# The first group of an attention block made on chip, and the modulations moved into that block's drain

## The chip, the cores and the metric

The kernel runs on one core of a Trainium2 chip. The metric is device microseconds (us) of one execution; three executions are summed up by their median. The profile is one further execution, recorded by the hardware profiler.

## The reference

The input is `x` of 16 x 128 x 256 (batch, channels D, positions T) and a mask `cond_2048` of 16 x 256. Two layers are added to `x` in turn; all arithmetic is float32.

```python
def _L0_cond_ref(x, mask, Wq, Wo):          # first layer
    xt = jnp.transpose(x, (0, 2, 1))
    q = xt @ Wq.T
    qh = q.reshape(B, T, NH, dk).transpose(0, 2, 1, 3)      # 8 heads of 16
    scores = scale * jnp.einsum('bhqd,bhkd->bhqk', qh, qh)
    logits = (scores * cmask + (1.0 - cmask) * NEG) * rmask
    attn = jax.nn.softmax(logits, axis=-1)
    ctx = jnp.einsum('bhqk,bhkd->bhqd', attn, qh)
    out = ctx.transpose(0, 2, 1, 3).reshape(B, T, D) @ Wo.T
    return jnp.transpose(out, (0, 2, 1))

def _L1_cond_ref(x, timestep_embed, ada_w, ada_b, ...):     # second layer
    ada = (timestep_embed @ ada_w + ada_b)[:, None, :]      # timestep_embed is the mask array
    shift1, scale1, gate1, shift2, scale2, gate2 = jnp.split(ada, 6, axis=-1)
    x1 = _ln(x) * (1.0 + scale1) + shift1
    ...                                     # 16 heads of attention, gate1, _ln, scale2, shift2, a gelu layer, gate2

x = x + _L0_cond_ref(x, cond_2048, L0_cond_Wq, L0_cond_Wo)
x = x + _L1_cond_ref(x, cond_2048, ...)
```

## The kernel before

The program has two blocks with a barrier between them. The first, `first_block`, is the first layer; the second, `layers`, is the second layer, in float32 products that are split into a high and a low part. The change touches only the first.

The first block works on 8 groups of two batch entries each. A group has 4 units; a unit is two heads (s = 0, 1) of both entries (b = 0, 1), so there are 32 units (`UNITS`). For a unit n the engines do:

- PE: `scores(n, b)` (L401) from the stacked rows `KS` and `QS` into the PSUM tensor `ring`; later `shift(n, b)` (L413), which adds the negative maxima through an identity; later `pv(n, kt)` (L425), the product of the exponentials with the values `V`, into `pair`.
- DVE: `maxima(n, b)` (L602), two reductions.
- ACT: `exponentials(n, b)` (L539), two activations into `pt`.

The stacked rows hold, for each head, three parts of 16 rows and a row (two in the layout) for the mask, so that one product over 49 rows gives queries times keys to float32 accuracy and the masking. They are made by a round trip: POOL multiplies x with the mask and splits the product in a high part `xh` and a low part `xl` (`masked(g)`, L333 to L340); PE projects them with Wq (`project(g)`, three products in L672); ACT copies the high part of the result (`queries(g)`, L522), DVE the low part (`low(g)`, L597); SP writes both to HBM (`gather(g)`, L262 and L264) and reads them back into the rows of `KS` and `QS` (`spread(g)`, six transfers in L280 for the queries, four in L273 for the mask rows). `values(g)` (L378, ACT L529) makes V.

A group's end is a tail that is spread over the following units: `sums` (ACT L549), transposes (PE L471), division by the sums (DVE L640, L647), transposes (L478), a copy (ACT L568), the product with Wo (L483) and the addition to `X` (DVE L656). For the last group there are no more units, so the tail stands alone; that end, with the first row norms of the second layer (`deviations`, `normal_rows`, L149 to L168, turned by PE in L116), is called the drain here.

Beside that the first block prepares the second one. SP loads the 12 chunks of the second layer's weights into `stage` (L288); ACT and POOL split each half chunk into `w_hi` (L573) and `w_lo` (L355), one half chunk in each of units 0 to 23. The modulations (`ada`, six vectors for every entry) are 24 products of 16 columns on PE (L387), in four parts: two ahead of the first scores and two in unit 0. `modulated` (L607 to L617) finishes them on DVE in unit 1. The weights of the modulations lie in `late` and in half of `pt`; therefore `exponentials` of units 0 and 1 and the first `sums` wait for all four parts (`pe_ada`).

Each engine runs its own instructions in program order; SP's are the loads and stores, all on one queue. The order is written out by hand: every engine has a loop over n in which the calls above stand. An instruction that waits holds back all that is behind it on its engine. The head of SP's list before the change is x[0:2], mask(0), Wq, the constants, cond, Wo, mask(1), x[2:4], the modulations' weights (1.5 MB), the mask rows, gather(0), the biases, spread(0), x[4:16] (1.5 MB), mask(2), gather(1), two weight chunks, and then per group `spread(g + 1)`, `mask(g + 3)`, `gather(g + 2)` and two weight chunks.

Of the kernel before, what the change touches and what calls it, by code (L numbers as in the profile page):

```python
# [12 lines left out]
P = 128  # L13
# [159 lines left out]
def first_block(nc, sem, sb, x, cond, Wq, Wo, ada_w, ada_b, qkv_w, qkv_b, out_b, ffn_b1, ffn_b2,  # L173
# [5 lines left out]
    LAST = 4 * (NGR - 1) + 8  # L179
    LQ, LG = 10 * 16, 3 * 16  # L180
    vbank, tbank = psum[0], psum[1]
    O = psum[2]
    with ExitStack() as ctx:
# [25 lines left out]
        first = pt[:, 0, :, :, :].rearrange("p a s n -> p (a s n)")  # L209
        wqo = first[:, 0:2 * P].rearrange("p (i n) -> p i n", i=2)  # L210
        cnd = first[0:B, 512:512 + DIM]
        bias_rows = first[0:BIASES, 1024:1024 + P]
        aw = [late[:, 0:6 * DIM], pt[:, 1, :, :, :].rearrange("p a s n -> p (a s n)")[:, 0:6 * DIM]]

        l_cst, l_small, l_w, l_x0, l_x1, l_x, l_ada = (sem(n) for n in (
            "l_cst", "l_small", "l_w", "l_x0", "l_x1", "l_x", "l_ada"))
# [22 lines left out]

        def tail_of(n, lag):  # L240

            g, r = divmod(n - lag, 4)
            return g if r == 0 and 0 <= g < NGR else None

        with nc.Block() as block:

            @block.sync
            def _(sp):
                def mask(g):

                    wait(sp, pool_x, g - 1)
# [3 lines left out]
                def gather(g):  # L255

                    q = qd[g % 2]
                    if g >= 2:
                        sp.wait_ge(l_q[g % 2], LQ * (g // 2))
                    sp.wait_ge(act_q1, g + 1)  # L260
                    for c in (0, 2):
                        sp.dma_start(q[:, c], qh[:, :].bitcast(F32)).then_inc(l_qd[g % 2], 16)  # L262
                    sp.wait_ge(dve_ql, g + 1)
                    sp.dma_start(q[:, 1], ql[:, :].bitcast(F32)).then_inc(l_qd[g % 2], 16)  # L264

                def spread(g):
# [9 lines left out]
                    sp.wait_ge(l_qd[g % 2], LG * (g // 2 + 1))  # L276
# [15 lines left out]
                sp.dma_start(wqo[:, 0, :], Wq).then_inc(l_w, 16)  # L292
                sp.dma_start(cst[:, :], consts).then_inc(l_cst, 16)
                sp.dma_start(cnd, cond).then_inc(l_w, 16)
                sp.dma_start(wqo[:, 1, :], Wo).then_inc(l_w, 16)
                mask(1)
                sp.dma_start(X[:, 2:4, :], x[2:4].rearrange("b p d -> p b d")).then_inc(l_x1, 16)
# [10 lines left out]
                sp.wait_ge(l_nb, 16)  # L308
                spread(0)
                sp.dma_start(X[:, 4:B, :], x[4:B].rearrange("b p d -> p b d")).then_inc(l_x, 16)  # L310
                mask(2)
                gather(1)
                weights(0)
                weights(1)
                for g in range(NGR):
                    if g + 1 < NGR:
                        spread(g + 1)
# [1064 lines left out]
```

## Time and profile before

| | us |
|---|---|
| median of 3 executions | 802.7 (802.21 to 804.07) |
| the profiled execution, its own time | 802.39 |
| its span, first to last instruction | 800.6 |
| first block, start to the barrier | 0 to 205.6 |
| first scores (unit 0) | 30.33 |
| first scores of unit 4 (group 1) | 58.24 |

PE is busy for 747.2 us of the span (93%), ACT for 436.6, DVE for 385.5 and POOL for 144.8. In a row of the time line the first number is the start, the second the time from there to the end of the last of the instructions that are merged in the row, then come engine, line, operation, the tile written and what it was made from, and the count. Brackets hold how long the engine was idle before it and what ended that.

### The profile page before, as it was taken

Reading aid. Unit: us, or ns where it says so; the run is one execution under the profiler, and the core shown is the slowest. Engines: PE = TensorE matmul, PEld = TensorE weight load, DVE = VectorE, ACT = ScalarE, POOL = GpSimd, SP = SyncE. Lnnn points to the kernel's source line nnn. Section 1 sums busy time; section 2 is a strip of 40 time slices with the busy share of each in tenths; the row PEclk is TensorE's granted clock in tenths of the full one; section 3 lists DMA queues with packets and bytes.
Section 4 is the critical chain, followed back from the end, with each engine's and each line's share of the span. In section 5 each row is a group of like instructions: output and inputs, shape, how many; then the busy total and the mean of one; then the engine's idle time right before and its main releaser. Section 6 shows DMA issues by size and latency. Waiting matters only on the chain.

```text
span 800.6 us, 12914 instructions
## 1 busy us (share of the span) xinstructions
PE 747.2 (93%) x4737; PEld 615.9 (77%) x4737; DVE 385.5 (48%) x782; ACT 436.6 (55%) x1189; POOL 144.8 (18%) x136
## 2 busy tenths in 40 slices
PE   3689999997699999999999999999999999899997
PEld 2555555554598888888888888888888888778886
DVE  1155666666234543444545444545444345545444
ACT  1056776765357454555564555565544566647553
POOL 4133444200033111111111111111111122200000
PEclk9999999999899999999999999999999999999999
DMA  6999988740433221221221221212222223220001
GB/s 196 244 155 188 200 206 192 138 64 1 131 119 103 69 80 68 66 79 67 67 80 66 66 75 59 76 66 65 79 80 66 80 93 105 80 79 31 29 21 53
DMA packets 68851, 75.69 MB, mean 95 GB/s; under 512 B 4040, under 2 KB 48064, under 8 KB 68800
## 3 DMA queue, kind: packets, MB, share of 16 engines
q1 hardware_dynamic: 68800, 75.01, 35.1%
q8 instruction: 32, 0.52, 0.3%
q14 instruction: 19, 0.16, 0.1%
HBM read 47.96 MB, written 27.03 MB: 94 GB/s over the span
## 4 chain that ended last, share of the span: by engine, by line
PE 69%; DVE 3%; ACT 2%; DMA 1%; issue 0%; DVEq 0%; SPq 0%; ACTq 0%
PE bank L672 27%; PE pair L672 14%; PE ring L672 13%; PE ring L958 7%; PE pair L944 6%; PE ring L116 1%; DVE x1l L1186 1%; ACT x1h L1046 1%; PE ring L977 0%; ACT probs L1065 0%; DMA x1f<-in_L_cond_ffn_w_dram 0%; PE ring L913 0%; DVE ol L1219 0%; DVE pB L1197 0%; DMA turned<-pB 0%
## 5 line engine op out<-in xcount | busy, mean ns | idle before, releaser
L1065 ACT ACTIVATE probs<-pair,nm 128x128 f32<-128x128 f32 x256 | 98.5, 486 | 183.1 <-DVE nm L1208 183.1
L1321 POOL TENSOR_TENSOR probs<-probs,rinv 128x512 f32<-128x512 f32 x64 | 66.7, 1042 | 356.6 <-DVE rinv L1216 356.6
L672 PE MATMUL bank<-x1h,w_hi 128*128 128x512 f32 x256 | 112.1, 438 | 5.6 <-DVE x1l L1186 5.5
L602 DVE TENSOR_REDUCE mx<-ring 128x2 fp32r<-128x512 f32 x128 | 80.1, 683 | 64.2 <-PE ring L401 64.2
L672 PE MATMUL bank<-x1l,w_hi 128*128 128x512 f32 x256 | 101.5, 396 | 0.0
L672 PE MATMUL bank<-x1h,w_lo 128*128 128x512 f32 x256 | 101.2, 395 | 0.0
L539 ACT ACTIVATE pt<-ring 128x512 f32<-128x512 f32 x128 | 70.1, 594 | 44.2 <-PE ring L413 44.0
L1239 DVE COPY Vv<-pair 128x512 f32<-128x512 f32 x64 | 44.2, 691 | 80.4 <-PE pair L672 80.4
L672 PE MATMUL pair<-w_hi,x1l 128*128 128x256 f32 x256 | 72.7, 284 | 0.0
L672 PE MATMUL pair<-w_lo,x1h 128*128 128x256 f32 x256 | 72.4, 283 | 0.0
L672 PE MATMUL pair<-w_hi,x1h 128*128 128x256 f32 x256 | 72.2, 282 | 0.0
L944 PEld LDWEIGHTS pair<-K,Q 128*128 128x128 f32 x512 | 67.0, 191 | 5.3
L958 PEld LDWEIGHTS ring<-pT,Vv 128*128 128x128 f32 x512 | 66.8, 191 | 5.1
L944 PE MATMUL pair<-K,Q 128*128 128x128 f32 x512 | 67.6, 275 | 0.0
L958 PE MATMUL ring<-pT,Vv 128*128 128x128 f32 x512 | 67.3, 274 | 0.0
L1219 DVE SCALAR_TENSOR_TENSOR ol<-ring,bias,oh 128x512 fp32r<-128x512 f32 x64 | 48.0, 750 | 32.2 <-ACT oh L1074 32.2
L1208 DVE TENSOR_REDUCE nm<-pair 128x4 f32<-128x512 f32 x64 | 43.7, 682 | 40.2 <-PE pair L944 40.0
L1216 DVE RECIPROCAL rinv<-sums 128x4 f32<-128x4 f32 x64 | 11.4, 178 | 102.4 <-ACT probs L1065 102.4
L672 PEld LDWEIGHTS bank<-x1h,w_hi 128*128 128x128 f32 x256 | 49.1, 192 | 12.8 <-issue 5.8
L672 PEld LDWEIGHTS bank<-x1h,w_lo 128*128 128x128 f32 x256 | 48.7, 190 | 11.0
L1065 ACT ACTIVATION_READ_ACCUMULATOR probs<-pair,nm 128x1 f32 x256 | 56.1, 219 | 0.0
L672 PE MATMUL ring<-oh,wo_hi 128*128 128x512 f32 x128 | 51.0, 399 | 3.5 <-DVE ol L1219 3.4
(175 smaller groups left out, 1476.0 us busy)
## 6 DMA issues: line engine op xcount, KB each, us to landing
turned<-pB SPq DMA_DIRECT2D x63, 256.0 KB, 2.0
pT<-turned SPq DMA_DIRECT2D x63, 256.0 KB, 2.8
QS<-qd SPq DMA_DIRECT2D x16, 384.0 KB
stage<-in_L_cond_qkv_w_dram SPq DMA_DIRECT2D x12, 512.0 KB, 7.6
qd<-qh SPq DMA_DIRECT2D x16, 256.0 KB
KS<-qd SPq DMA_DIRECT2D x16, 256.0 KB
mb<-in_cond_dram SPq DMA_DIRECT2D x8, 256.0 KB, 10.4
qd<-ql SPq DMA_DIRECT2D x8, 256.0 KB
```

The lines of the kernel that those rows point to most:

```text
L116: last = nc.tensor.transpose(bank[:, (2 * k + b) * P:(2 * k + b + 1) * P], xn(2 * half + b)[:, k * P:(k + 1) * P], ident)
L539: nc.scalar.activation(pt[:, n % 2, b, s, :], ring[:, 2 * b + s, :], ACT.Exp, scale=DK ** -0.5).then_inc(act_exp, 1)
L602: dve.tensor_reduce(mx[:, 2 * b + s, :], ring[:, 2 * b + s, :].rearrange("p (k q) -> p k q", k=2), AX_X, ALU.max, negate=True).then_inc(dv ...
L672: last = nc.tensor.matmul(bank, w(k), x(k), start=(start and i == 0), stop=(stop and i == len(terms) - 1))
L944: last = nc.tensor.matmul(Sb[:, t], Q[:, h % 2, t], K[:, h % 2, t], start=True, stop=True)
L958: last = nc.tensor.matmul(Ob[:, b * T:(b + 1) * T], V[:, ho // 2 % 2, b, h % 2 * DH:(h % 2 + 1) * DH], pT[:, h % 2, :, b, :], start=True, ...
L1065: last = nc.scalar.activation(plain(probs)[:, t] if direct else probs[:, :, b, :].rearrange("p c a -> p a c"), Sb[:, t] if direct else Sb[ ...
L1208: dve.tensor_reduce(nm[:, h % 2, :], Sb[:, :].rearrange("p (b k) -> p b k", b=GB), AX_X, ALU.max, negate=True).then_inc(dve_mx, 1)
L1216: dve.reciprocal(rinv[:, h % 2, :], sums[:, h % 2, :]).then_inc(dve_ri, 1)
L1219: dve.scalar_tensor_tensor(ol[:, :], Ob[:, :], qkvb[:, 2, ho:ho + 1], oh[:, :].bitcast(F32), ALU.add, ALU.subtract).then_inc(dve_ol, 1)
L1239: dve.tensor_copy(V[:, hn // 2 % 2, 2 * (hn % 2):2 * (hn % 2) + 2, :], Vb[:, :].rearrange("p (b d) -> p b d", b=2)).then_inc(dve_v, 1)
L1321: pool.tensor_tensor(w, w, r, ALU.mult).then_inc(pool_p, 1)
```

## The change

- Group 0 takes no round trip. DVE multiplies x[0:2] with the mask and splits it (`x0m`, `x0h`, `x0l`). ACT and DVE copy each head's 16 columns of Wq three times into a stack `ws_h`, `ws_l` of 8 x 64 columns. PE's new `stack(j)` gives the stacked rows of unit j directly: four products of 512 columns into `pair`, the first of which puts the mask row in; ACT makes `h0` from it, and two operations of DVE write `QS` and `KS`. `stack(0)` stands ahead of the first scores, `stack(n + 1)` in units 0 to 2. Ahead of them PE runs 6, 4 and 3 products with zeros.
- `gather(0)`, `spread(0)` and `masked(0)` are gone. `project(1)` and `values(0)` stand in unit 0, with their parts on ACT and DVE.
- Wq, the constants, cond and Wo are loaded from ACT's queue. x comes in four loads, [0:2], [2:4], [4:8] and [8:16], of which the last stands behind `spread(1)`.
- The weight splits are done in units 2 to 25 (`SPLIT0 = 2`); one weight chunk is loaded between `mask(g + 3)` and `gather(g + 2)`, the other one behind it.
- All four parts of the modulations and the turn of the biases stand behind the last product with V (n == UNITS), `modulated` one step later on DVE. Their weights and the biases are loaded at the end of SP's list, into `stage`, `xm` and half of `V`, when those are free.

```diff
+        x0h, x0l, ws_h, ws_l, one_h, zero, h0, mbr = (
+            w_hi[:, 6144 + 512 * i:6144 + 512 * (i + 1)] for i in range(8))
...
                 def mask(g):
 
-                    wait(sp, pool_x, g - 1)
+                    wait(sp, pool_x, g - 2)
+                    if g == 2:
+                        sp.wait_ge(dve_x0, 1)
+                        sp.wait_ge(act_mbr, 1)
...
-                for k in range(KT):
-                    sp.dma_start(aw[k], ada_w[k * P:(k + 1) * P, :]).then_inc(l_ada, 16)
                 sp.wait_ge(pool_nb, 1)
                 sp.dma_start(rowd.rearrange("t b d -> b t d"), rows[:, :, :]).then_inc(l_nb, 16)
-                gather(0)
+                sp.dma_start(X[:, 4:8, :], x[4:8].rearrange("b p d -> p b d")).then_inc(l_x2, 16)
+                mask(2)
+                gather(1)
+                weights(0)
+                sp.wait_ge(l_nb, 16)
+                spread(1)
+                sp.dma_start(X[:, 8:B, :], x[8:B].rearrange("b p d -> p b d")).then_inc(l_x, 16)
+                weights(1)
+                for g in range(NGR):
+                    if g and g + 1 < NGR:
+                        spread(g + 1)
+                    if g + 3 < NGR:
+                        mask(g + 3)
+                    if g and 2 * g + 1 < CHUNKS:
+                        weights(2 * g + 1)
+                    if g + 2 < NGR:
+                        gather(g + 2)
+                    if 2 * g + 2 < CHUNKS:
+                        weights(2 * g + 2)
+                sp.wait_ge(pool_lo, 2 * CHUNKS)
+                sp.dma_start(aw[0][0], ada_w[0:P, :]).then_inc(l_ada, 16)
...
+                sp.wait_ge(pool_x, NGR - 1)
+                sp.dma_start(aw[1][1], ada_w[P:2 * P, 8 * P:12 * P]).then_inc(l_ada, 16)
+                sp.wait_ge(pe_pv, 4 * (NGR - 1))
+                sp.dma_start(aw[1][0], ada_w[P:2 * P, 0:8 * P]).then_inc(l_ada, 16)
...
+                def zeros(count):
+
+                    for i in range(count):
+                        nc.tensor.matmul(ring[:, 0, :], zero[:, 0:P], zero, start=True, stop=True)
+
+                def stack(j):
+
+                    bank = O[:, min(j, 1), :]
+                    w = slice(j * P, (j + 1) * P)
...
+                    nc.tensor.matmul(bank, one_h[:, 0:P], mbr, start=True, stop=False)
...
+                    nc.tensor.matmul(bank, ws_h[:, w], x0h, start=False, stop=False)
...
+                    nc.tensor.matmul(bank, ws_l[:, w], x0h, start=False, stop=False)
...
+                    nc.tensor.matmul(bank, ws_h[:, w], x0l, start=False, stop=True).then_inc(pe_st, 1)
...
                 for n in range(LAST + 1):
                     if n < UNITS:
                         scores(n, 0)
-                    if n == 0:
-                        modulations(2)
                     if 0 <= n - 1 < UNITS:
                         shift(n - 1, 1)
+                    if n == 0:
+                        pe.wait_ge(act_set, 1)
+                        pe.wait_ge(dve_set, 1)
+                        project(1)
+                    if n < 3:
+                        stack(n + 1)
...
+                    if n == UNITS:
+                        pe.wait_ge(act_exp, 4 * UNITS)
+                        pe.wait_ge(l_small, 80)
+                        nc.tensor.transpose(ring[:, 1, 12 * B:12 * B + BIASES], bias_rows, ident[0:BIASES, 0:BIASES])
+                        pe.wait_ge(l_ada, 48)
+                        for part in range(4):
+                            modulations(part)
...
+                def stack(j):
+
+                    act.wait_ge(pe_st, j + 1)
+                    wait(act, dve_st, j)
+                    nc.scalar.activation(h0, O[:, min(j, 1), :], ACT.Identity, bias=cols[:, 1:2],
+                                         scale=cols[:, 0:1]).then_inc(act_h, 1)
...
+                def stack(j):
+
+                    dve.wait_ge(act_h, j + 1)
+                    h, bank = h0.bitcast(F32), O[:, min(j, 1), :]
+                    dve.scalar_tensor_tensor(QS[:, 0, j, :], h, cols[:, 2:3], bank, ALU.mult, ALU.add)
+                    dve.scalar_tensor_tensor(KS[:, 0, j, :], h, cst[:, C_AK:C_AK + 1], bank, ALU.mult,
+                                             ALU.add).then_inc(dve_st, 1)
```

PE's order up to the second half of unit 0's scores, before. `bank` is the PSUM bank of projections and modulations, L401 the scores:

```order
L435 MATMUL bank<-cst,pt 128x128 x2
L437 MATMUL bank<-cst,pt 128x16 x2
L672 MATMUL bank<-xh,wq_h 128x512
L672 MATMUL bank<-xl,wq_h 128x512
L672 MATMUL bank<-xh,wq_l 128x512
L378 MATMUL bank<-wT,X 128x128 x4
...
L446 MATMUL bank<-cst,pt 128x72
L387 MATMUL bank<-cndT,late 128x16
...
L401 MATMUL ring<-QS,KS 128x256 x4
```

And in the changed kernel (L411 are the products with zeros, L420 to L430 a stack, L446 the scores, L790 project(1)):

```order
L411 MATMUL ring<-w_hi 128x512 x6
L481 MATMUL bank<-cst,pt 128x128
L411 MATMUL ring<-w_hi 128x512 x4
L484 MATMUL ring<-cst,pt 128x128
L486 MATMUL ring<-cst,pt 128x16 x2
L411 MATMUL ring<-w_hi 128x512 x3
L420 MATMUL pair<-w_hi 128x512
L424 MATMUL pair<-w_hi 128x512
L427 MATMUL pair<-w_hi 128x512
L430 MATMUL pair<-w_hi 128x512
L446 MATMUL ring<-QS,KS 128x256 x4
L790 MATMUL bank<-xh,wq_h 128x512
```

The projection, the values and twelve of the modulation products have left the place ahead of the first scores; zeros and one stack stand there.

SP's list from the mask rows on, in the changed kernel:

```order
L314 DMA rowd<-rows 16x2x256
L315 DMA X<-in_x_dram 128x4x256
L272 DMA mb<-in_cond_dram 128x512
L281 DMA qd<-qh 8x16x512 x2
L283 DMA qd<-ql 8x16x512
L307 DMA stage<-in_L_cond_qkv_w_dram 128x1024
L292 DMA QS<-rowd 1x4x512 x2
...
L299 DMA QS<-qd 48x4x512
L321 DMA X<-in_x_dram 128x8x256
L307 DMA stage<-in_L_cond_qkv_w_dram 128x1024
L272 DMA mb<-in_cond_dram 128x512
L281 DMA qd<-qh 8x16x512 x2
```

The first pair of gather and spread in it belongs to group 1; no 1.5 MB load stands ahead of it any more, and 1 MB of x and a weight chunk stand behind it, ahead of gather(2).

PE's order in the drain, in the changed kernel (L470 the products with V, L514 and L521 the tail's transposes, L116 the turn of the normalized rows, L526 the product with Wo):

```order
L470 MATMUL pair<-pt,V 32x256 x8
L549 MATMUL ring<-cst,stage 128x72
L404 MATMUL ring<-cndT,stage 128x16
L404 MATMUL ring<-cndT,V 128x16
...
L404 MATMUL ring<-cndT,xm 128x16
L514 MATMUL bank<-cst,late 128x128 x4
L116 MATMUL bank<-cst,mb 128x128 x4
L116 MATMUL ring<-cst,mb 128x128 x4
L514 MATMUL bank<-cst,late 128x128 x4
L521 MATMUL bank<-cst,late 128x128 x4
L526 MATMUL bank<-late,wT 128x512
```

Before, the first L514 (then L471) followed the products with V directly; the 25 rows between are new there.

## Rows read from the trace of the kernel before

**Rows 1.** The page: TensorE's busy tenths in 40 slices of the span.
```profile
PE   3689999997699999999999999999999999899997
```

**Rows 2.** Time line of the start: spread(0), first scores, first weight split.
```profile
18.13 0.92 SPq L280 DMA_DIRECT2D KS<-qd  x2
...
30.33 0.79 PE L401 MATMUL ring<-QS,KS 49*128 49x256 f32 x4 [5.94 <-DMA QS<-qd]
...
40.22 0.62 ACT L573 CAST w_hi<-stage 128x512 fp32r<-128x512 f32 x1 [21.54 <-DMA stage<-in_L_cond_qkv_w_dram]
```

**Rows 3.** Time line, PE: the first scores of units 4, 8 and 12.
```profile
58.24 0.50 PE L401 MATMUL ring<-QS,KS 49*128 49x256 f32 x4
...
79.13 0.50 PE L401 MATMUL ring<-QS,KS 49*128 49x256 f32 x4
...
98.45 0.50 PE L401 MATMUL ring<-QS,KS 49*128 49x256 f32 x4
```

**Rows 4.** Time line of the drain, PE, DVE and ACT.
```profile
195.35 1.07 PE L425 MATMUL pair<-pt,V 128*32 128x256 f32 x16
...
199.74 0.66 PE L116 MATMUL bank<-cst,mb 128*128 128x128 f32 x4 [2.73 <-DVE mb L168]
...
204.63 0.69 DVE L656 TENSOR_TENSOR X<-bank,X 128x512 f32<-128x512 f32 x1 [2.55 <-PE bank L483]
...
205.63 1.51 ACT L1031 ACTIVATE x1f<-bank,ada 128x128 f32<-128x128 f32 x4 [2.21 <-PEq L245]
```

**Rows 5.** Time line of the start: durations on POOL, ACT and DVE.
```profile
4.52 1.26 POOL L333 TENSOR_TENSOR xm<-X,mb 128x512 f32<-128x512 f32 x1 [4.08 <-DMA mb<-in_cond_dram]
...
9.73 0.59 ACT L522 CAST qh<-bank 128x512 fp32r<-128x512 f32 x1 [2.58 <-PE bank L672]
...
18.71 0.69 DVE L597 TENSOR_TENSOR ql<-bank,qh 128x512 fp32r<-128x512 f32 x1 [7.67 <-ACT qh L522]
```

**Rows 6.** Time line, PE: products at the slow level, and the first fast one.
```profile
11.19 2.05 PE L378 MATMUL bank<-wT,X 128*128 128x128 f32 x8 [1.49 <-DVE ql L597]
...
14.57 0.63 PE L672 MATMUL bank<-xl,wq_h 128*128 128x512 f32 x1
...
14.99 0.63 PE L672 MATMUL bank<-xh,wq_l 128*128 128x512 f32 x1
...
42.60 1.22 PE L413 MATMUL ring<-identr,mx 128*128 128x256 f32 x4
...
44.66 1.08 PE L425 MATMUL pair<-pt,V 128*32 128x256 f32 x8 [0.84 <-ACT pt L539]
...
51.09 0.39 PE L672 MATMUL bank<-xh,wq_l 128*128 128x512 f32 x1
```

**Rows 7.** Stretches: busy us by engine (count), granted clock, DMA share, GB/s.
```profile
80.00:90.00 10.00, 8.84 (x76) 5.14 (x76) 6.86 (x14) 6.79 (x13) 4.98 (x5) 1.00 0.91 197
...
210.00:212.00 2.00, 2.00 (x6) 1.54 (x6) 0.00 (x0) 0.00 (x0) 0.00 (x0) 0.50 1.03 326
```

**Rows 8.** The page's groups: busy, mean ns of one, idle before.
```profile
L1219 DVE SCALAR_TENSOR_TENSOR ol<-ring,bias,oh 128x512 fp32r<-128x512 f32 x64 | 48.0, 750 | 32.2 <-ACT oh L1074 32.2
```

**Rows 9.** Time line: two like operations of DVE, and POOL's beside them.
```profile
44.99 0.19 DVE L613 TENSOR_TENSOR gb<-ada,bias 128x32 f32<-128x32 f32 x1
45.10 1.27 POOL L355 TENSOR_TENSOR w_lo<-stage,w_hi 128x512 fp32r<-128x512 f32 x1 [2.92 <-ACT w_hi L573]
45.22 1.20 DVE L615 TENSOR_TENSOR gb<-ada,bias 128x32 f32<-128x32 f32 x1
```

**Rows 10.** Time line, SP's queue: the first of spread(7)'s transfers.
```profile
157.68 0.91 SPq L280 DMA_DIRECT2D KS<-qd  x2
```

**Rows 11.** Stretches, as in rows 7: where that spread ends.
```profile
168.00:169.00 1.00, 1.00 (x13) 0.46 (x12) 0.44 (x1) 1.00 (x2) 0.00 (x0) 1.00 0.68 102
169.00:170.00 1.00, 1.00 (x11) 0.69 (x7) 1.00 (x3) 0.05 (x1) 0.00 (x0) 1.00 0.11 18
```

**Rows 12.** Time line, PE: the first and last products of modulation parts 0, 1.
```profile
19.15 0.54 PE L387 MATMUL bank<-cndT,late 128*128 128x16 f32 x2
...
23.80 0.59 PE L387 MATMUL bank<-cndT,pt 128*128 128x16 f32 x2
```

More of the change, by code:

```diff
@@ L179, in first_block @@
     LAST = 4 * (NGR - 1) + 8
+    SPLIT0 = 2
     LQ, LG = 10 * 16, 3 * 16
@@ L307, in _ @@
                     row += n
[L308 to L317, printed above, removed]
-                    if g + 3 < NGR:
-                        mask(g + 3)
-                    if g + 2 < NGR:
-                        gather(g + 2)
-                    for c in (2 * g + 2, 2 * g + 3):
-                        if c < CHUNKS:
-                            weights(c)
+                sp.wait_ge(pool_x, NGR - 1)
+                sp.dma_start(aw[1][1], ada_w[P:2 * P, 8 * P:12 * P]).then_inc(l_ada, 16)
+                sp.wait_ge(pe_pv, 4 * (NGR - 1))
+                sp.dma_start(aw[1][0], ada_w[P:2 * P, 0:8 * P]).then_inc(l_ada, 16)
             @block.gpsimd
@@ L372, in values @@
                 def values(g):
-                    taken = min(g + 2, NGR) if g else 1
+                    taken = min(g + 1, NGR - 1)
                     wait(pe, act_q1, taken)
@@ L544, in sums @@
                     wait(act, pe_pv, 4 * g + 2 * half + 2)
-                    if g == 0:
-                        act.wait_ge(pe_ada, 4)
-                    else:
+                    if g:
                         wait(act, pe_oT, 2 * g + half - 1)
                     nc.scalar.copy(oT[:, half, :], O[:, half, :]).then_inc(act_o, 1)
-                queries(0)
-                values(0)
-                queries(1)
+                act.wait_ge(dve_zero, 5)
+                stack(0)
                 for n in range(LAST + 1):
@@ L556, in _ @@
                         exponentials(n - 1, 1)
+                    if n == 0:
+                        queries(1)
+                    if n < 3:
+                        stack(n + 1)
                     if n % 4 == 2 and n // 4 + 2 < NGR:
@@ new lines, in _ @@
+                TINY = 2.0 ** -12
+                dve.memset(zero.bitcast(F32), 0.0).then_inc(dve_zero, 1)
+                dve.memset(w_hi[:, 7168:8192].bitcast(F32), 0.0).then_inc(dve_zero, 1)
+                dve.memset(one_h[:, 0:P].bitcast(F32), 0.0).then_inc(dve_zero, 1)
+                dve.wait_ge(dve_zero, 3)
+                ones = one_h[:, 0:P].bitcast(F32).rearrange("p (s r) -> p s r", s=2)[:, :, ROWS_ONE:ROWS_ONE + 1]
+                dve.memset(ones, TINY / P).then_inc(dve_zero, 1)
@@ L629, in _ @@
                         maxima(n, 0)
-                    if n == 1:
-                        modulated()
+                    if n == 0:
+                        low(1)
+                    if n < 3:
+                        stack(n + 1)
                     if n % 4 == 2 and n // 4 + 2 < NGR:
```

203 lines of the change are left out of this document (125 added, 78 removed).

## Prediction

> **What bounds the kernel now.** I first read the page's busy line by tenths of the span: TensorE works nearly throughout, and only the first block (the first ten of 40 slices) has holes, at its start and its end [rows 1]. Then I read the time line of that block, from its start, for what ended each wait. The first scores start at 30.33 us and wait there for DMA: spread(0), issued from 18.13 on, took until then [rows 2]. What stands before 30 us is one round trip of the first queries through HBM. A second wait follows: ScalarE stands in front of its first weight split until 40.22 us, because the load of the weights is queued behind everything else, and the exponentials of unit 0 are behind that split in program order [rows 2]. So unit 4, the first of group 1, starts only at 58.24 us. From there a group takes 20.9 us (58.24 to 79.13) and then 19.3 (79.13 to 98.45) [rows 3]; nothing in this steady part waits for a spread. The block ends in a drain: the last products with V from 195.35 on, the normalized rows turned at 199.74, the last addition to X at 204.63; at 205.63 all engines pass to the second block [rows 4], which the change leaves alone. What group 0 saves is therefore worth its full size at the end, if the later groups keep their pace, less what is added to the drain.
>
> **Group 0 up to its first scores.** Removed: gather(0), spread(0), the POOL part masked(0). Added: a chain PE, ACT, DVE. The four loads that now go through ACT's queue start at once; the row nearest to them is POOL's first product, which had its two inputs at 4.52 with the same kind of loads in flight [rows 5]. I take Wq and the constants at about 4 us, x and its mask at 4.8. Then: transpose of Wq and its end, 4.6; ScalarE's ws_h, at most the 0.59 of a 512-column copy, 5.2; VectorE's ws_l, at most the 0.69 of a 512-column operation [rows 5], 5.8; x0m, x0h and x0l, 0.69 each at most, 7.8. Beside this TensorE runs 13 zero products of 512 columns, which start 0.42 us apart at the slow level, 1.2 GHz [rows 6], 5.5 us in all, and the transposes of Wo and the conditions; started at 1.4 (after one memset of 512 columns, which has no row on VectorE and is taken as no more than 0.69), it is through them at 8.4. (The level is told by durations, 0.63 against 0.39; the granted clock shows it as 0.50 where it has fallen before [rows 7].) So the zeros hide VectorE's chain, and not the other way round. stack(0) is four such products: 10.1, its result seen at 10.3. ScalarE's h0 0.59 [rows 5]: 11.0. Two scalar_tensor_tensor of 0.75 [rows 8]: 12.6. First scores at **12.7** instead of 30.33.
>
> One thing lies in the way: VectorE's x0m and x0l run while POOL makes masked(1). In the trace, two like operations of VectorE differ: 0.19 us alone, and 1.20 when started 0.12 after a POOL product of 1.27, ending with it [rows 9]. By this row one VectorE step can be held 1.3 us; the zeros cover that much (9.7 is when TensorE wants x0l, 7.8 when it is ready). If two steps are held, scores start at 13.4. The Trainium skill, SBUF — State Buffer, "Who interferes with whom", says that a VectorE operation with two SBUF inputs and a GpSimd one that reads SBUF exclude each other for the whole operation, whichever starts first; by that rule the total would be up to 0.7 us above mine. The trace agrees in the one place where it shows it.
>
> **Units 0 to 3.** At the fast level a normal unit takes 4.8 (19.3 / 4) [rows 3]. Units 0 to 2 now also hold stack(n+1): four products on TensorE, one h0 on ScalarE (0.59; the weight split of the same size leaves units 0 and 1) and 1.5 on VectorE, which has to be done before the next scores and stands between the two pairs of maxima. I add 0.6 for each, since VectorE, with four maxima of 0.65 and these 1.5, is then the tightest engine: 5.4. Unit 0 also has project(1), queries(1), low(1) and values(0), mostly at the slow level: 6.6. Unit 2 has project(2), queries(2) and low(2): 5.9; unit 3 values(1): 5.5. Sum 23.4, so unit 4 could start at 36.1.
>
> Its rows must be there. gather(1) is issued when queries(1) is done, 15.4, and low(1), 16.1; nothing is in flight then but x[4:8] and a mask, so its 768 KB are written by 20.5. spread(1) takes 11.5 us, as the last spread does when it is alone: issued 157.68, the transfer gone in the slice 169 to 170 [rows 10, 11]. It lands at 32, four before it is wanted. Unit 4 starts at **36.1** instead of 58.24: **22.1 us gained**. Its weights are in front too: weights(0) goes out before spread(1), so ScalarE's wait of 21.54 [rows 2] is gone; what is late next is weights(1) with 1 MB of x ahead of it, wanted only in unit 4.
>
> **Group 1 and after.** spread(2) follows 1.75 MB of x, weights and mask and the 768 KB of gather(2), behind spread(1); at the 326 GB/s of a plain load [rows 7] these take 5 and 3 us: 32 + 5 + 3 = 40, landing at 53 with weights(2) ahead. Unit 8 asks at 36.1 + 19.3 = 55.4. So it just fits; the margin is 2.4. Later spreads are issued at the same place of a group as now (the split that the second load waits for has moved by two units, and the order of the loads with it). The 20.9 of group 1 hold 1.6 over the steady 19.3; I count half of that as gone, **0.8**. Units 24 and 25 now hold a weight split each (0.59 to 0.62 on ScalarE), of which I count **0.5** on the path.
>
> **The drain.** Added on TensorE behind the last product: the transpose of the biases (0.3) and 24 products of 16 columns. At the slow level such a product starts every 0.43 (19.15 to 23.80: the first and the last of twelve rows of two records each, a product a row) [rows 12], 10.3 us in all; at the fast level half, 5.2. They are hidden only by the hole before 199.74, where TensorE waits 2.73 for the normalized rows [rows 4], and then in part, since the turn of group 7's first half, which now comes after them, has its partner on VectorE: 195.35 + 1.0 + 0.3 + 5.2 = 201.8 for the end of the products, 202.3 for that turn, 203.0 for its VectorE part. Then VectorE makes the modulations, seven small steps of 0.19 or somewhat more [rows 9] with a wait between them, 1.7 us without POOL beside it, up to 204.7; the second half's VectorE part ends at 205.4. From that end to the last addition VectorE idles 2.55 now [rows 4] (transpose, ScalarE's copy, product) and the addition takes 0.69: 208.6 for 205.3, **3.3 us lost**. At the slow level 8.5 would be lost. The last product leaves TensorE at the fast level, and the small ones came in the trace only at the slow one, so I take **4.5**. Their loads (ada in three pieces, five of biases) wait for the last split, for masked(7) and for unit 27, all over 15 us before: nothing.
>
> Sum, on the profiled execution of 802.39 (0.3 below the median of 802.7): 802.39 - 22.1 - 0.8 + 0.5 + 4.5 = **784.5**. To put both ends: without any gain in group 1, with the drain at 8.5, 789.3; with units 0 to 3 at 4.8 each, so that unit 4 starts as its rows land, at 32, and with the drain at 3.3, 779.2.
>
> **Rivals.**
> *A, TensorE stays at the slow level through group 0.* For: after the zeros it has nothing to do for 2.4 us while ScalarE and VectorE finish stack(0); and in the trace the first 512-column product of 0.39 comes at 51.09 [rows 6]. Against: it came there after six us without a hole, 44.66 on, and from 12.7 on the new order has no hole either. Price: scores 0.79 [rows 2], shift 1.22, products with V 1.08 [rows 6], twice each, is 6.2, and a stack 1.7; with two projections of 1.3 and two value products of 2.05 [rows 6], without unit 0's products with V, 34.6 for four units by durations, some 31 by starts (a row's end lies some 0.1 behind the next one's start): unit 4 at 43.7, **792**.
> *B, the wait moves from group 0 to group 1.* spread(1) or spread(2) lands later than asked. For: DMA is busy 0.91 in the steady part [rows 7], and the margin at unit 8 is small. Past the margin each us late is one us of time; with spread(2) 8 to 10 late, **790 to 792**. This is also the case on the other side: if spread(1) lands no sooner than spread(1) of before, just ahead of 58.24, then group 0's gain is all waited away and the drain's 4.5 and the 0.5 remain, **807**. It decides from a landing at 53 on, 21 later than I work out. Against: 3 MB (x and ada) that stood before it in the queue are behind it now.
> *C, the modulations in the drain run at the slow level.* In the trace products of 16 columns came at the slow level alone [rows 12]. Price 8.5 for 4.5: **788.5**.
> *D, the first scores come as late as before*, the change not doing what it says: nothing in the order makes them wait for HBM any more; not given a chance of its own.
>
> **How the numbers follow.** Forecast (779 to 788) 0.60; A 0.13; B up to 795 0.09, B past the point 0.03; C 0.13; better than 779, 0.02. Predicted 784.5. The range, 779 to 793, takes in the forecast with its ends, C, A at its price and most of B. A measurement of this kernel can tell about 0.2% (1.6 us) from no change: faster by more 0.96, within 0.01, slower 0.03.
>
> **What would show it.** Right: first scores at 12 to 14 us; unit 4 at 34 to 39 with its idle time ended by ScalarE or VectorE, not by DMA; a start of unit 8 some 19 to 20 later; the 16-column products right behind the last product with V, 5 to 7 us long; the second block some 17 to 19 earlier than 205.63. Wrong: scores of unit 4 or 8 released by DMA (B); 512-column products still 0.42 apart after 20 us (A); 16-column products 0.43 apart in the drain (C); anything else in the second block than a shift.

## The result and the profile after

The changed kernel takes 791.39 us (median of 4 runs, 789.09 to 792.2) beside 802.46 for the kernel before on the same chip: ratio 0.9839, interval 0.9806 to 0.9872. The profiled execution took 792.2 us, span 790.0. Forecast were 784.5 and 779 to 793: right in sign, inside the range, 6.9 us too low, and outside the 779 to 788 of the forecast without its rivals. Lines of after: scores L446, stack L420 to L430, modulations L404.

The page's busy tenths, against [rows 1]:
```profile
PE   7799999986999999999999999999999999899997
```
Of the hole at the start a shallow one is left; the one at the end of the first block is still there.

The start, time line, against [rows 2, 5, 8]:
```profile
5.98 0.47 PE L481 MATMUL bank<-cst,pt 128*128 128x128 f32 x1 [1.59 <-DMA cst<-stack_constants]
...
8.19 2.20 DVE L730 CAST w_hi<-pt 128x512 fp32r<-128x512 f32 x1
...
8.84 1.26 POOL L353 TENSOR_TENSOR xm<-X,mb 128x512 f32<-128x512 f32 x1
...
10.07 0.63 PE L420 MATMUL pair<-w_hi 128*128 128x512 f32 x1
...
10.43 0.98 DVE L732 TENSOR_TENSOR w_hi<-pt,w_hi 128x512 fp32r<-128x512 f32 x1
...
12.35 0.78 ACT L575 ACTIVATE w_hi<-pair,cols 128x512 fp32r<-128x512 f32 x1 [4.33 <-PE pair L430]
...
14.62 0.50 PE L446 MATMUL ring<-QS,KS 49*128 49x256 f32 x4 [2.37 <-DVE KS L700]
```
The constants come at 5.98, VectorE's cast of x0h takes 2.20 while POOL works beside it, and the first scores start at 14.62 instead of 30.33.

Group 1's rows, SP's queue and PE, and the starts of units 8 and 12 [rows 3]:
```profile
18.07 0.62 SPq L283 DMA_DIRECT2D qd<-ql  x1
...
24.94 0.81 SPq L299 DMA_DIRECT2D KS<-qd  x2
...
38.95 0.50 PE L446 MATMUL ring<-QS,KS 49*128 49x256 f32 x4 [3.70 <-DMA QS<-qd]
...
60.96 0.51 PE L446 MATMUL ring<-QS,KS 49*128 49x256 f32 x4
...
79.78 0.50 PE L446 MATMUL ring<-QS,KS 49*128 49x256 f32 x4
```
TensorE was ready for unit 4 at 35.25 and waited 3.70 for its rows. Group 1 then takes 22.0 (38.95 to 60.96), longer than the 20.9 before; the stretches (columns as in [rows 7]) show the clock there:
```profile
35.00:40.00 5.00, 1.30 (x16) 0.83 (x8) 1.51 (x3) 0.28 (x2) 0.50 (x1) 0.99 1.10 228
40.00:45.00 5.00, 4.17 (x28) 1.88 (x26) 1.73 (x4) 3.08 (x6) 1.27 (x2) 0.50 0.91 346
45.00:50.00 5.00, 5.00 (x30) 3.38 (x26) 2.37 (x6) 2.43 (x5) 4.39 (x4) 0.50 0.57 174
50.00:55.00 5.00, 5.00 (x43) 3.18 (x43) 3.32 (x6) 3.27 (x7) 0.27 (x1) 0.99 1.04 157
```
After the idle stretch the granted clock is 0.50 for ten us. From unit 8 on a group takes 18.8 (60.96 to 79.78), the last 18.3; before it was 18.3 to 19.3.

The drain, against [rows 4]:
```profile
175.78 1.07 PE L470 MATMUL pair<-pt,V 128*32 128x256 f32 x16
...
179.54 0.37 PE L404 MATMUL ring<-cndT,stage 128*128 128x16 f32 x2
...
180.16 0.59 PE L404 MATMUL ring<-cndT,stage 128*128 128x16 f32 x2
...
184.43 1.09 PE L514 MATMUL bank<-cst,late 128*128 128x128 f32 x4
...
190.75 2.07 PE L526 MATMUL bank<-late,wT 128*128 128x512 f32 x2 [0.68 <-ACT late L641]
...
192.86 0.69 DVE L772 TENSOR_TENSOR X<-bank,X 128x512 f32<-128x512 f32 x1 [3.96 <-PE bank L526]
...
197.84 0.77 PE L790 MATMUL bank<-x1h,w_hi 128*128 128x512 f32 x1 [5.02 <-DVE x1l L1304]
```
The stretches:
```profile
175.00:180.00 5.00, 5.00 (x47) 3.66 (x46) 3.73 (x17) 1.68 (x4) 0.00 (x0) 0.98 0.00 0
180.00:190.00 10.00, 9.13 (x42) 8.39 (x41) 3.02 (x14) 0.00 (x0) 0.00 (x0) 0.50 0.00 0
```
The modulations start 0.22 apart and from 179.7 on 0.43 apart. The last addition to X stands 17.1 behind the last products with V; before it was 9.3, with the granted clock at 1.00 throughout. The second block's first product (209.61 before) starts 11.8 earlier, the span ends 10.6 earlier.

### The profile page after: what moved, and what is told of

The parts are those of the page before. It is cut to its first block, busy times and chain, and to the rows that moved or that the text cites. A ratio compares the mean times of both kernels' runs of the same rounds, so it can differ in the third digit from the quotient of the medians.

```text
span 790.0 us, 12978 instructions
## 1 busy us (share of the span) xinstructions
PE 756.6 (96%) x4763; PEld 621.5 (79%) x4763; DVE 394.5 (50%) x801; ACT 439.5 (56%) x1194; POOL 142.5 (18%) x133
## 4 chain that ended last, share of the span: by engine, by line
PE 70%; DVE 3%; ACT 2%; DMA 1%; issue 0%; DVEq 0%; SPq 0%; ACTq 0%
PE bank L790 27%; PE pair L790 14%; PE ring L790 13%; PE ring L1076 7%; PE pair L1062 7%; PE ring L116 1%; DVE x1l L1304 1%; ACT x1h L1164 1%; PE ring L1095 0%; ACT probs L1183 0%; DMA x1f<-in_L_cond_ffn_w_dram 0%; PE ring L1031 0%; DVE ol L1337 0%; DVE pB L1315 0%; DMA turned<-pB 0%
## 5 line engine op out<-in xcount | busy, mean ns | idle before, releaser
L790 PE MATMUL bank<-x1h,w_hi 128*128 128x512 f32 x256 | 112.1, 438 | 5.6 <-DVE x1l L1304 5.5
L790 PE MATMUL bank<-x1l,w_hi 128*128 128x512 f32 x256 | 101.5, 396 | 0.0
L790 PE MATMUL bank<-x1h,w_lo 128*128 128x512 f32 x256 | 101.3, 396 | 0.0
L790 PE MATMUL pair<-w_hi,x1l 128*128 128x256 f32 x256 | 72.8, 284 | 0.0
L790 PE MATMUL pair<-w_lo,x1h 128*128 128x256 f32 x256 | 72.6, 283 | 0.0
L790 PE MATMUL pair<-w_hi,x1h 128*128 128x256 f32 x256 | 72.3, 282 | 0.0
L790 PEld LDWEIGHTS bank<-x1h,w_hi 128*128 128x128 f32 x256 | 49.1, 192 | 13.6 <-issue 6.6
L790 PEld LDWEIGHTS bank<-x1h,w_lo 128*128 128x128 f32 x256 | 48.6, 190 | 11.0
L458 PEld LDWEIGHTS ring<-identr,mx 128*128 128x128 f32 x256 | 37.6, 196 | 22.7 <-issue 13.4
```

The lines of the kernel that those rows point to most:

```text
L458: last = nc.tensor.matmul(out, mx[:, 2 * b + s, qt:qt + 1].to_broadcast([P, P]), identr[:, None, :].to_broadcast([P, 2, P]), start=False, ...
L790: last = nc.tensor.matmul(bank, w(k), x(k), start=(start and i == 0), stop=(stop and i == len(terms) - 1))
```

## The experiments

Each kernel is the changed one with the edit shown. Times are given by the ratio to the kernel before on the same chip, to be held against 0.9839; most intervals overlap with its own, so what decides is the trace, and where two ratios don't overlap this is said. A spread's time is counted from its first issue (L299 in the changed kernel), which is when its gather has landed, to the end of TensorE's wait (in c2, where TensorE doesn't wait, to the end of SyncE's). The four kernels under "All together" are called c1 to c4, in their order.

**POOL held back.**
```
 def masked(g):
     wait(pool, pool_x, g - 1)
+    if g == 1:
+        pool.wait_ge(dve_x0, 3)
```


> GpSimd's mask product and splits of group 1 wait until VectorE has finished its own split of group 0's rows; nothing else is changed. Theory (the cast that took 2.20 us on VectorE was held up by GpSimd's work beside it): the cast falls to 0.3 to 0.9 us, the low part from 0.98 to 0.7 or less, and the first scores start at 13.2 to 13.9 instead of 14.62; group 1's projection may then wait for GpSimd, to 15.5. The time falls by 0 to 1 us only if the rows of group 1 are not what group 1 waits for; since they are, 791 to 791.5. Rival (the cast waits for something else, the page's duration is not a conflict): it stays above 1.8 us and the first scores at 14.6.

Ratio 0.9791 (0.9735 to 0.9848). The time line's cast, first scores:
```profile
7.91 0.50 DVE L732 CAST w_hi<-pt 128x512 fp32r<-128x512 f32 x1
...
13.37 0.50 PE L448 MATMUL ring<-QS,KS 49*128 49x256 f32 x4 [2.37 <-DVE KS L702]
```
The cast falls from 2.20 to 0.50, the first scores come 1.25 earlier, and POOL's part ends when it did (12.6). The expectation that nothing reaches the end was wrong: the gather starts 1.25 earlier too, the rows land at 35.90 after a wait of 2.05, and unit 8 starts at 56.83, 4.1 earlier. Of the 3.05 by which the rows land earlier the earlier gather explains 1.25; the spread took 12.2 instead of 14.0 with the same transfers in the same order, and no run shows why. First scores differ too among the seven kernels that have the changed kernel's start (14.00 to 14.62), so that the hold's price lies between 0.6 and 1.25.

**Order of SyncE's loads.**
```
+sp.dma_start(X[:, 8:B, :], ...)
+weights(0)
+weights(1)
 gather(1)
-weights(0)
 sp.wait_ge(l_nb, 16)
 spread(1)
-sp.dma_start(X[:, 8:B, :], ...)
-weights(1)
```


> SyncE's order alone: the load of X[8:16] and the first two weight chunks are issued ahead of the gather of group 1 instead of among and behind its transfers; they then fall into the stretch 10 to 17 in which the queues stand idle. Theory (the rows of group 1 land late because the transfers compete): they land by 34 to 36 instead of 38.9, the wait of TensorE ahead of group 1 shrinks from 3.7 to under 1 us, the clock doesn't fall at 40, group 1 takes 19 to 20 us instead of 22.0, and the time falls by 4 to 6 us, to 785.5 to 787.5. Rival (the spread of the stacked rows is slow by itself, 2 KB rows into few partitions): it lands at 37 or later, the gain is under 2 us, time 789.5 or more.

Ratio 0.9799 (0.9744 to 0.9855). Time line, PE:
```profile
38.24 0.50 PE L446 MATMUL ring<-QS,KS 49*128 49x256 f32 x4 [2.14 <-DMA QS<-qd]
```
Unit 4 still waits 2.14; the rival is right, the spread took 13.4 from its issue at 24.86 with the loads out of its way.

**Zero products in the wait.**
```
+if n == 4:
+    pe.wait_ge(act_exp, 4 * 3 + 2)
+    zeros(14)
 if n < UNITS:
     scores(n, 0)
```


> 14 products with the zero tile are added ahead of group 1's first scores, in the time in which TensorE waits there for the rows; nothing else is changed. Theory (the idle wait, not the wait's length, lets the clock fall at 39.9): the granted clock of 40 to 50 is near 1 instead of 0.50, group 1 takes 19 to 20 us instead of 22.0, and unit 8's first scores come 2 to 3 us earlier than 60.96, with the time at 788.5 to 789.5. Rival (group 1 is held by the transfers of group 2's rows, whatever the clock): unit 8's first scores stay at 60 to 61 and the time at 791 to 792.

Ratio 0.9815 (0.9767 to 0.9863). The clock is 1.00 from 40 to 45 but falls after it (0.78 and 0.53 in the next two stretches of 5 us), and group 1 takes 22.8: ScalarE stood 1.46 us in front of a weight split whose chunk was queued behind 1 MB of x (1.44 in the changed kernel, at 42.92). So I repeated it with the two loads swapped:
```
-sp.dma_start(X[:, 8:B, :], ...)
 weights(1)
+sp.dma_start(X[:, 8:B, :], ...)
```


> The changed kernel with the 14 products with the zero tile ahead of group 1, as in the run that added them alone, and SyncE's second weight chunk issued ahead of X[8:16] instead of behind it. Theory (that run gained little because ScalarE, in its in-order queue ahead of the exponentials, then waited 1.46 us for that chunk, and the clock fell in the idle time that followed): no wait of ScalarE for a weight chunk in group 1, the clock near 1 from 40 to 55, group 1 in 19 to 20.5 us instead of 22 to 22.8, and the time 788 to 789. Rival (group 1 is bound by something else, as group 2's rows): ScalarE's wait goes, and group 1 still takes 21.5 us or more, time 790 to 792.

Ratio 0.9846 (0.9793 to 0.9898). Stretches, and unit 8's first scores:
```profile
40.00:45.00 5.00, 4.06 (x37) 2.47 (x38) 2.93 (x5) 3.37 (x7) 1.18 (x1) 1.00 0.93 331
45.00:50.00 5.00, 4.55 (x43) 2.98 (x42) 3.64 (x9) 3.66 (x8) 4.45 (x5) 1.00 0.74 187
```
```profile
60.26 0.50 PE L446 MATMUL ring<-QS,KS 49*128 49x256 f32 x4 [2.12 <-DMA QS<-qd]
```
No wait of ScalarE, the upper clock throughout, and group 1 needs 18.7 of its own (39.41 to 58.14). Of the gain in group 1, 2.12 is waited away at unit 8: the theory was right for group 1, the rival for the time.

**No zeros at the start** (`zeros(6)`, `zeros(4)` and `zeros(3)` taken out).

> The 13 products with the zero tile at the start are left out. Theory (they raise the clock, and are otherwise hidden): the products of the first stack run at the lower level, about 0.43 each and more instead of 0.21 to 0.43, units 0 to 3 run slow at their start, unit 4's first scores come at the time of the rows anyway (38.5 to 39.5) since group 1 waits for them, and the time is the same within 1 us, 790.5 to 792.5. Rival (they hold TensorE's queue longer than VectorE's chain): the first scores come up to 0.7 us earlier than 14.62, and the gather with them.

Ratio 0.9864 (0.9839 to 0.9888); first scores 14.04, unit 4 at 39.31. The start:
```profile
8.26 0.50 DVE L727 CAST w_hi<-pt 128x512 fp32r<-128x512 f32 x1
...
8.80 2.02 DVE L729 TENSOR_TENSOR w_hi<-pt,w_hi 128x512 fp32r<-128x512 f32 x1
...
10.87 0.80 PE L430 MATMUL pair<-w_hi 128*128 128x512 f32 x1 [0.77 <-DVE w_hi L729]
```
Here POOL holds VectorE's two-input step (2.02) and not the cast (0.50), and the stack's last product waits for VectorE. With the zeros VectorE is what that product's weights wait for last, too (0.45, to 11.46). So this run doesn't show that the zeros hold stack(0) back: 14.04 lies among the 14.00 to 14.62 of the seven kernels with zeros. Nothing of it reaches unit 4, as the theory said.

**No modulations.**
```
-for part in range(4):
-    modulations(part)
+nc.tensor.matmul(ring[:, 1, 0:12 * B], adaw(0, 0), X[:, 0, 0:12 * B], ...).then_inc(pe_ada, 4)
```


> The 24 modulation products of the first block's drain are left out: one product of 192 columns writes that tile instead, so the modulations are wrong and the rest of the work is unchanged. Theory 1 (their whole cost lies on the path, at the lower clock): the first block's last X add comes about 7 us earlier after the last values product than the 17.1 us of the changed kernel, and the time falls from 791.4 to 784 to 785. Rival (the drain waits for VectorE's normalised rows, ready at 180.1, and for the last group's chain anyway): the add comes only 3 to 4 us earlier, time 787 to 788. A second question: whether the clock still falls near 180 without the products of 16 columns. If they pull it down, the transposes and the output product behind them run at the upper level; if TensorE's own idle time does, they still run at the lower one.

Ratio 0.9763 (0.9716 to 0.9809). The drain:
```profile
184.78 2.07 PE L526 MATMUL bank<-late,wT 128*128 128x512 f32 x2 [0.68 <-ACT late L641]
...
186.89 0.69 DVE L772 TENSOR_TENSOR X<-bank,X 128x512 f32<-128x512 f32 x1 [3.96 <-PE bank L526]
```
The addition stands 11.3 behind the last products with V (175.60): the modulations cost 5.8 of the 17.1, nearer to theory 1 than to the rival. The output product is 2.07 here too, and the granted clock is 0.50 from 181.6 on: it falls in the drain without them as well, here behind 2.29 us in which TensorE waits (to 179.99). So 2.0 of the 7.8 that the drain lost against the kernel before are left without any modulation.

**The drain's order.**
```
 if n == UNITS:
-    pe.wait_ge(l_ada, 48); parts 0 to 3
 if n == UNITS + 1:
+    pe.wait_ge(l_ada, 48); parts 0 to 2
     pe.wait_ge(dve_n1, 1)
+if n == UNITS + 2: part 3, ahead of L521 (VectorE: modulated() here)
```
(In words, not in code.)

> Only the order of the drain is changed: the transposes of the last group's first half come ahead of the modulations, three quarters of the modulations stand where TensorE otherwise waits for VectorE's normalised rows (to 180), the last quarter where it waits for the second half's context rows, and VectorE turns them into scales one step later, while TensorE and ScalarE finish the group. Theory (the modulations cost what they cost because the group's chain stands behind them): from the last values product to the last X add 12.5 to 14.5 us instead of 17.1, and the time 3 to 4 us less, 787.5 to 788.5. Rival (what counts is the lower clock of the drain, whatever the order): the same products at 0.43 each, 16 us or more, time 790 to 791.

Ratio 0.9785 (0.9761 to 0.9809). The drain's end:
```profile
176.15 1.07 PE L470 MATMUL pair<-pt,V 128*32 128x256 f32 x16
...
191.80 0.69 DVE L773 TENSOR_TENSOR X<-bank,X 128x512 f32<-128x512 f32 x1 [1.96 <-PE bank L528]
```
The addition stands 15.65 behind, between the two: order gives 1.4, with the products at 0.43 from 180.35 on. That the low clock keeps the rest is borne out by c2 below, where the same order takes 12.2.

**Products at the start of the second block.**
```
+for i in range(10):
+    nc.tensor.matmul(Sb[:, :], w_hi[:, 0:P], w_hi[:, 0:512], start=True, stop=True)
 pe.wait_ge(act_m1, 1)
```


> The changed kernel with 10 products into a free bank at the start of the second block, in the 4 us in which TensorE waits there for its first rows; the drain is left as it is. Theory (the clock is low when the block begins because TensorE stood idle before it, and about half of the 5.8 us until it rises is lost): the first projections run at 0.22 to 0.23 each instead of 0.43, the stretch from the second block's first product to the end is 2 to 3 us shorter than 592.2, and the time 788.5 to 789.5. Rival (after the drain's low clock ten products at 0.43 don't raise it): the clock still rises 4 us or more into the block, time 791 to 792.

Ratio 0.9806 (0.9755 to 0.9858). Time line, PE:
```profile
197.76 0.63 PE L790 MATMUL bank<-x1h,w_hi 128*128 128x512 f32 x1
...
199.44 0.40 PE L790 MATMUL bank<-x1l,w_hi 128*128 128x512 f32 x1
```
The upper level comes 1.7 us into the block instead of 5.8, and from the first product to the end it is 588.5 instead of 592.2. Only about half of these 3.7 stands at the start: product for product the two traces are 1.8 apart after 5.5 us and 2.2 after 61. Another 1.4 comes at 689 to 695, where the changed kernel's products with 512 columns are 0.43 apart for some 3 us and this kernel's aren't, a place that the edit doesn't touch. And 0.45 is given back: the first product stands 5.43 behind the last addition to X instead of 4.98, behind the added ones.

**All together.** The start alone: POOL's wait, `project(1)` ahead of `scores(0, 0)`, and on SyncE `weights(0)`, `weights(1)`, the copies of the stacked rows, then the gather, and `sp.wait_ge(l_q[1], LQ)` ahead of the next mask and gather.

> Three edits that all bring group 1's rows forward: GpSimd's wait of the run before (no cast of 2.20 us), group 1's projection ahead of the first scores, and SyncE's order: two weight chunks and the stacked rows' four copies into each tile issued before the gather, the second gather and the third mask held until the spread has landed. Theory (rows of group 1 late through their own chain and through transfers that compete): they land by 32 to 34, no wait ahead of group 1, no fall of the clock there, unit 8's first scores at 53 to 55 instead of 60.96, and 784 to 786 in all, unless group 2's rows, now asked for later, are late in their turn: then unit 8 waits 1 to 3 us and the time is 786 to 788. Rival (the spread takes its 10 us and more whatever runs beside it): unit 4's first scores at 35 or later, time 787 or more.

Ratio 0.9778 (0.9746 to 0.9809). Time line, PE:
```profile
35.03 0.50 PE L455 MATMUL ring<-QS,KS 49*128 49x256 f32 x4 [2.04 <-DMA QS<-qd]
```
The rival, since the spread took 13.3 from 21.77 on. With the drain's order and the ten products added:

> The three edits of the kernel before it in this list, the drain's new order, and 10 products into a free bank at the start of the second block, whose only use is to keep TensorE at work until its first rows are ready. If the parts add up: 4 to 7 us from the start, 3 to 4 from the drain, and 2 to 3 from a second block that starts at the upper clock: 777 to 782. If the clock falls in the drain whatever is done, 782 to 785; if the added products delay the second block's first product (they end after its rows are ready), 1 us more.

**Ratio 0.9694 (0.9672 to 0.9716), 779.29 us**, better than both kernels beyond the intervals. Unit 8, the drain and the second block's first products:
```profile
56.10 0.50 PE L455 MATMUL ring<-QS,KS 49*128 49x256 f32 x4 [2.86 <-DMA QS<-qd]
...
172.11 1.07 PE L479 MATMUL pair<-pt,V 128*32 128x256 f32 x16
...
177.43 0.59 PE L413 MATMUL ring<-cndT,xm 128*128 128x16 f32 x2
...
180.96 0.37 PE L413 MATMUL ring<-cndT,stage 128*128 128x16 f32 x2
...
184.33 0.69 DVE L783 TENSOR_TENSOR X<-bank,X 128x512 f32<-128x512 f32 x1 [0.56 <-PE bank L538]
...
189.32 0.47 PE L801 MATMUL bank<-x1h,w_hi 128*128 128x512 f32 x1 [1.43 <-DVE x1l L1317]
...
189.63 0.39 PE L801 MATMUL bank<-x1l,w_hi 128*128 128x512 f32 x1
```
The block starts at the upper level. No wait stands ahead of unit 4 in this trace; unit 8 waits 2.86, to 56.10 (and unit 12 another 0.76).

Of the 13.1 by which the span is shorter than the changed kernel's, 3.7 stand at the last products with V, 4.9 in the drain and 4.6 behind it. The drain takes 12.2, not the 15.65 of the run with the same order alone, because the granted clock is low only from 177 to 180.5 here and back at 1.00 when the last quarter of the modulations runs. The mean granted clock is 0.990 to 0.994 in all five executions, 0.970 to 0.978 in the four of the changed kernel. What brings the level back in this drain (and in c3's, 12.2 too) and not in others (13.4 in c4), no run shows; so the gain goes with the clock, and it isn't shown which edit keeps the clock up.

Two attempts on unit 8's wait failed.

`SPLIT0 = 6`, X[8:16] behind the second gather, a hold on `l_q[0]` ahead of the third:

> The best of the kernels so far (group 1's rows forward, the drain's order, the products at the start of the second block) with less beside the spreads of groups 1 and 2: X[8:16] goes behind the spread of group 1, the gather of group 3 and the mask of group 4 wait until the spread of group 2 has landed, and the weight splits stand four units later again, in units 6 to 29, their loads likewise. Theory (the spread of a group's rows lasts as long as the transfers beside it make it): the spread of group 1 lands by 33 and that of group 2 by 53 instead of 56.1, the wait of 2.9 us ahead of unit 8 goes, and the time falls by 2 to 3 us to 776 to 777.5. Rival (a spread takes its 10 us by itself, and the holds only move the lack to group 3): 779 or more.

Ratio 0.9801 (0.9755 to 0.9846). Unit 8:
```profile
62.76 0.58 PE L458 MATMUL ring<-QS,KS 49*128 49x256 f32 x2 [7.91 <-DMA QS<-qd]
```
The spread of group 1, with nothing behind it, took 13.3 (22.82 to 36.12): there the theory fell. That of group 2 took 17.9 (from 44.84), the longest of all, also with nothing issued behind it. But this edit put X[8:16] ahead of it (issued at 38.91), and that 1 MB took 14.6 us to land, until about 53.5. So for group 2 this run is no test of the theory, and whether X[8:16] made the spread that long stays open.

The best kernel without its hold:

> The best of the kernels so far (ratio 0.9694 to the kernel before) without its hold: SyncE no longer waits for the landing of group 1's rows before it issues the next mask and the gather of group 2. Theory (from the last issue of a spread to its landing it takes 9.5 to 11.3 us whatever runs beside it, and 10.5 with the fewest transfers beside it, so that the hold brought group 1 nothing and made group 2 late): group 1's rows land within 1 us of 34.3, those of group 2 by 50, the wait of 2.9 us ahead of unit 8 goes, and the ratio falls by 2 to 3 us to 0.966 to 0.967. Rival (the hold did shorten the spread of group 1): its rows land at 36 or later, TensorE waits 1.5 us or more there and the clock falls with it, ratio 0.970 or more.

Ratio 0.9756 (0.9731 to 0.9782). Time line, PE:
```profile
35.96 0.70 PE L454 MATMUL ring<-QS,KS 49*128 49x256 f32 x4 [2.26 <-DMA QS<-qd]
```
The clock fell (0.50 from 40 to 45), unit 8 didn't wait. The rival's numbers came out; the ratio is clear of the changed kernel's and of c2's, though c4 ran on another chip than c2. The rival's reason isn't shown by them: the spread took 14.1 here and 12.7 in c2 with the hold, but also 13.3 with the hold in c1 and 12.2 without one where POOL was held back. And only 0.7 us of the 3.4 between the two traces stand at the last products with V (172.85 against 172.11). The rest is the drain and the second block at the lower clock.

## Why the prediction was right, and where it was short

The sign and the place of the gain were right: group 0's round trip is gone, and from unit 8 on the groups keep their pace. The time is inside the range because that took in rivals A to C, and in part by luck: without the 1.9 that groups 2 to 7 gained against the forecast it would have been 793.3. Against the profiled execution the gain was 10.2, forecast 17.9. The missing 7.7, by its steps:

**First scores, 12.7; measured 14.62.** Two terms. "Wq and the constants at about 4 us" was 5.98. And the lock: "that the zeros cover" counted VectorE's two-input steps only, with 0.7 at most. It was the one-input cast between them that was held, and the run that holds POOL back prices it at 0.6 to 1.25. The Trainium skill, SBUF — State Buffer, "Who interferes with whom", also names copies and casts in a two-port mode; the trace agrees, 2.20 beside POOL's product and 0.50 with that product held back. I had applied half of the rule. A small third term is h0, 0.78 instead of 0.59.

**Units 0 to 3, 23.4; measured 20.6** (14.62 to 35.25): 2.8 better. Unit 1, which has a stack and no projection, took 4.6 instead of 5.4, so the stack's 0.6 was too much. The wait behind unit 3 swallowed all of it.

**"It lands at 32, four before it is wanted": this step failed.** It landed at 38.95, 3.7 after. Of the 7.0: the gather was issued 2.0 later (18.07 for 16.1), took 6.9 instead of 4.4, and the spread 14.0 instead of 11.5. This is rival B in small, at group 1 and not at group 2, and its sign (scores of unit 4 released by DMA) came. Part of the last 2.5 is the ruler: 11.5 ends where the DMA share falls, and in c3, with nothing behind the spread, the share falls between 34 and 35, some 12 after the issue, while TensorE goes on at 36.12 only. Taken to the end of TensorE's wait, spread(0) of [rows 2] had 12.2 already. The gather took 4.9 in c2, where weights(0) goes out ahead of it and not between it and the spread. That the transfers behind it lengthen a spread was my first cause, and no run bears it out: in twelve kernels group 1's took 12.2 to 14.2, and 13.3 with nothing behind it; what scatters it by 2 us stays open. The Trainium skill, SBUF — State Buffer, "Door 1: The DMA port swizzle", gives 104 GB/s at 1 MiB for 16 partitions, 189 for 32 and 196 for 64. A spread writes 1.5 MB into 16, 32 and 48 partitions at a time, by these an estimate of 9 us. The trace has more, 11.3 from the last issue (27.65) to 38.95 and 14.0 from the first. Unit 4 gained 19.3 for 22.1.

**Group 1, "0.8" gained; measured 1.1 lost.** The wait brought the clock down, which the sum had nowhere. The pair of runs with zero products shows it, for the two causes together: without the fall and without ScalarE's wait for weights(1), which the prediction named as next and gave no price, group 1 takes 18.7. It shows as well that most of the 3 us would have been lost at unit 8, which then waits 2.12.

**Groups 2 to 7, 0.5 lost; measured 1.4 gained** (unit 8 18.2 earlier, the last products with V 19.6). Not tried why.

**The drain, 4.5; measured 7.8** (19.6 gained ahead of it, 11.8 at the addition to X). Forecast and rival C mixed: half of the products ran fast, the rest and the chain behind at the slow level, near C's 8.5. Without the modulations 2.0 of the 7.8 are left, at a granted clock of 0.50 that the drain before didn't have; neither the sum nor C had that. The step that failed is "the last product leaves TensorE at the fast level": it did, and the level went 3 us later with TensorE busy throughout.

**The second block, "leaves alone":** 1.2 was lost between its start and the end of the span, and 0.4 lies outside the span. The level rises 5.8 us into it, against 5.2, which by the starts of like products costs 0.3. From there to 660 the changed kernel is up to 0.9 better, and at 688.5 to 692 it loses 1.7, at products 0.43 apart where the kernel before has 0.23; what brings the level down there wasn't looked into. The ten products gained 3.7, some 2 of it at the start.

Rivals A and B's far end did not come: products of 512 columns are 0.22 to 0.24 apart in unit 0 already, if only for a while.

## What to carry to other kernels

When a long wait is taken away, look for the next arrival on the same engine and cost its whole chain, from issue to landing, with rows that write the same partitions. An idle stretch on TensorE can cost twice, as time and as the low clock behind it: the waits ahead of group 1 of 2.0 to 3.7 us in nine traces here were all followed by 0.50, that of 0.99 in c3 wasn't, nor was that of 2.86 ahead of unit 8 in c2, nor the 2.73 in the drain of the kernel before [rows 4]. Products that fill it pay only if nothing later waits for DMA anyway. Small changes of this kind were worth little one by one and 1.5% together (0.9839 to 0.9694), much of it because the clock stayed up.

## What was not expected of the hardware

- A one-input cast from SBUF to SBUF on VectorE is held by POOL as a two-input operation is: 2.20 against 0.50. Which of the two is held differs: without the zeros it was the two-input step behind the cast (2.02 against 0.76 with POOL held back).
- The granted clock fell while TensorE was busy without a hole, in products of 16 columns: 0.98 in 175 to 180, 0.50 in 180 to 190. These products aren't needed for a fall (the drain without them has one), and in c2 they don't prevent a rise: starts are 0.22 apart again from 180.7 on.
- A granted 1.00 doesn't always say that products run at the upper level. In the kernel before it reads 1.00 from 30 to 40, where four score products take 0.79 [rows 2]. Without the zeros, stack(1)'s products start 0.43 apart (16.21, 16.64, 17.06) in this stretch of that kernel:
```profile
14.00:18.00 4.00, 3.96 (x12) 3.06 (x13) 2.26 (x5) 0.59 (x1) 2.38 (x3) 1.00 0.00 0
```
